# A spectral convolution with spline layers: who issues the copies of the modes

## The reference

```python
v  = groupnorm(x, 32 groups)                       # per image
ft = rfft2(v)
o[:, :, :16, :16]  = einsum('bixy,ioxy->boxy', ft[:, :, :16, :16],  w1)   # complex weights
o[:, :, -16:, :16] = einsum('bixy,ioxy->boxy', ft[:, :, -16:, :16], w2)
y  = irfft2(o) + einsum('bchw,oc->bohw', v, conv_w) + conv_b
y  = kan_linear(kan_linear(y, k1...), k2...)       # silu base + cubic splines over the channels
out = x + gelu(y)
```

## Time and profile before

| | us |
|---|---|
| median of 3 runs (3949.63 to 3950.17) | 3949.87 |
| the profiled execution, its own time | 3944.76 |
| its span in the trace | 3942.7 |
| TensorE busy | 3777.6 |
| VectorE busy | 3545.2 |
| ScalarE busy | 3421.6 |

### The profile page before, as it was taken

One profiled execution on the slowest core, in us unless ns is written; L12 is line 12 of the kernel. 1 busy time (PEld: TensorE's weight loads), 2 busy tenths in 40 slices (PEclk: granted clock), 3 DMA queues, 4 the chain that ended last, 5 costly groups with the idle time before them and its releaser, 6 DMA issues.

```text
span 3942.7 us, 102047 instructions
## 1 busy us (share of the span) xinstructions
PE 3777.6 (96%) x37098; PEld 2804.4 (71%) x37098; DVE 3545.2 (90%) x3979; ACT 3421.6 (87%) x3528; POOL 110.8 (3%) x132
## 2 busy tenths in 40 slices
PE   4995988999999999999999999999999999999998
PEld 2553944777777777777777777777777777777775
DVE  5774127999999999999999999999999999999996
ACT  1541227999999999999999999999999999999996
POOL 0000000000000000000000000000000000000000
PEclk9997999999999999999999999999999999999999
DMA  5996862322222332222222222322223222222322
GB/s 148 271 246 117 154 196 74 70 69 69 61 61 69 69 69 65 62 63 69 69 69 64 61 65 69 69 69 63 61 66 69 69 69 60 61 69 69 69 64 49
DMA packets 325155, 333.00 MB, mean 84 GB/s; under 512 B 86656, under 2 KB 255360, under 8 KB 323072
## 3 DMA queue, kind: packets, MB, share of 16 engines
q1 hardware_dynamic: 306688, 265.40, 24.9%
q0 software_dynamic: 18432, 67.12, 10.8%
HBM read 239.90 MB, written 88.08 MB: 83 GB/s over the span
## 4 chain that ended last, share of the span: by engine, by line
PE 83%; DVE 0%; issue 0%; ACT 0%; POOL 0%; POOLq 0%; ACTq 0%; DVEq 0%
PE l_ps L1092 78%; PE y_ps L1079 3%; PE y_ps L1071 2%; DVE cube2l L968 0%; DVE cube3r L968 0%; ACT above L1007 0%; ACT offset L1022 0%; ACT size L1018 0%; ACT S L1011 0%; ACT below L1015 0%; DVE cube1r L968 0%; DVE cube1l L968 0%; DVE cube0l L968 0%; ACT L1011 0%; DVE cube0r L968 0%
## 5 line engine op out<-in xcount | busy, mean ns | idle before, releaser
L1022 ACT ACTIVATE offset<-size 128x1024 f32<-128x1024 f32 x1280 | 1241.2, 1045 | 8.1
L1092 PE MATMUL l_ps<-S,kan_w 64*64 64x512 f32 x2048 | 358.2, 592 | 8.0 <-issue 8.0
L968 DVE SCALAR_TENSOR_TENSOR cube0r<-below,offset 128x1024 f32<-128x1024 f32 x256 | 312.1, 1219 | 58.5 <-ACT offset L1022 57.7
L1092 PE MATMUL l_ps<-below,kan_w 64*64 64x512 f32 x2048 | 359.2, 591 | 0.0
L1092 PE MATMUL l_ps<-cube3r,kan_w 64*64 64x512 f32 x2048 | 357.4, 589 | 0.8 <-DVE cube3r L968 0.8
L1092 PE MATMUL l_ps<-cube0r,kan_w 64*64 64x512 f32 x2048 | 358.0, 590 | 0.0
L1092 PE MATMUL l_ps<-cube0l,kan_w 64*64 64x512 f32 x2048 | 357.5, 589 | 0.0
L1092 PE MATMUL l_ps<-cube1l,kan_w 64*64 64x512 f32 x2048 | 357.5, 589 | 0.0
L1092 PE MATMUL l_ps<-cube1r,kan_w 64*64 64x512 f32 x2048 | 357.5, 589 | 0.0
L1092 PE MATMUL l_ps<-cube3l,kan_w 64*64 64x512 f32 x2048 | 357.4, 589 | 0.1
L1092 PE MATMUL l_ps<-inner_cube,kan_w 64*64 64x512 f32 x2048 | 357.4, 589 | 0.0
(11 more groups left out here) (129 smaller groups left out, 8106.6 us busy)
## 6 DMA issues: line engine op xcount, KB each, us to landing
img<-in_x_dram SPq DMA_DIRECT2D x128, 512.0 KB, 6.8
x_ring<-in_x_dram SPq DMA_DIRECT2D x256, 256.0 KB, 4.0
act_out<-in_x_dram POOLq DMA_DIRECT2D x128, 512.0 KB, 6.8
out_dram<-act_out SPq DMA_DIRECT2D x128, 512.0 KB, 2.6
rows_scratch<-rows SPq DMA_DIRECT2D x16, 1024.0 KB, 6.2
rows_t<-rows_scratch SPq DMA_DIRECT2D x512, 32.0 KB, 5.5
mix_w<-in_spec_w_r_dram SPq DMA_DIRECT2D x2, 2048.0 KB, 24.9
mix_w<-in_spec_w_i_dram SPq DMA_DIRECT2D x2, 2048.0 KB, 33.6
```

What stands on the lines that cost most here:

```text
L968: nc.vector.scalar_tensor_tensor(out=cube[q][side][:], in0=distance[layer][:], scalar=EDGE - KNOTS[q], in1=offset[layer][q][:], op0=ALU.mi ...
L1022: nc.scalar.activation(offset[layer][q][:], size[layer][:], ACT.Square, bias=-KNOTS[q]).then_inc(offset_ready[layer], 1)
L1092: ins = nc.tensor.matmul(dst[cols, r * MM:(r + 1) * MM], kan_w[layer][rows_, f, :], src[rows_, n * MM:(n + 1) * MM], start=(f == 0), stop= ...
```

## The change

The four DMAs A, B, C and D are taken out of SyncE's list and put at the head of ScalarE's list in the same block, in the same order and with the same semaphores. SyncE keeps the loads r0, i0, r1, i1. Nothing else differs.

```diff
         @block.sync
         def _(sp):
             sp.dma_start(pick_sb[:], t["pick"]).then_inc(pick_loaded, 16)
-            for k, ss in enumerate((slice(0, S_BANK), slice(S_BANK, NS))):
-
-                for part in range(2):
-                    src = modes[0:C, ss, :, part * MODES:(part + 1) * MODES, :]
-                    dst = modes[C:P, ss, :, (1 - part) * MODES:(2 - part) * MODES, :]
-                    sp.dma_start(dst.rearrange("p s g k b -> p (s g) (k b)"),
-                                 src.rearrange("p s g k b -> p (s g) (k b)")).then_inc(t["modes_doubled"][k], 16)
+            for k in range(2):
                 for part in range(2):
                     load_mix_part(nc, t, k, part, 0, C)
...
         @block.scalar
         def _(act):
+            for k, ss in enumerate((slice(0, S_BANK), slice(S_BANK, NS))):
+                for part in range(2):
+                    src = modes[0:C, ss, :, part * MODES:(part + 1) * MODES, :]
+                    dst = modes[C:P, ss, :, (1 - part) * MODES:(2 - part) * MODES, :]
+                    nc.scalar.dma_start(dst.rearrange("p s g k b -> p (s g) (k b)"),
+                                        src.rearrange("p s g k b -> p (s g) (k b)")).then_inc(t["modes_doubled"][k], 16)
             act.wait_ge(var_ready, 1)
             nc.scalar.activation(root[:], var[:], ACT.Sqrt).then_inc(root_ready, 1)
```

## The result

The changed kernel takes 3935.07 us (median of 7 runs, 3932.40 to 3940.25), the kernel before 3949.63 beside it (median of 7, 3943.62 to 3950.18). The ratio is 0.9968, with a 95% interval of 0.9956 to 0.998: 12.6 us less, from 8 to 17. The forecast was 3938.9. Times of the kernel before lie in two groups, near 3944 and near 3950, and its profiled execution (3944.76) is of the lower one; so the step by step account goes by the profiled executions, 3944.76 before and 3932.68 after.

The account below looks back on a forecast made before the run. It took the DMA engines' rate to bound `statistics`, through the landing of i1. Hiding r0's 12.0 us beside the copies, less 1.0 of friction, gave 3949.87 - 11.0 = 3938.9 us, range 3936.5 to 3950.5.

Parts of the forecast that it names:

- The bound: End of `statistics`: SyncE's issue of i1 comes last, released 17.9 us before i1 lands; the DMA rate bounds the stage.
- i and half of the r ahead of it: SyncE's issues in `statistics`: SyncE is released when this much transfer is still to come, 17.8 to 17.9 us.
- The rate: DMA in `statistics`: each half of the partitions takes some 180 to 190 GB/s of writes, both at once some 300.
- 276 GB/s: Copies beside r0 in `statistics`: the summed rate if each engine takes turns, r0 passing within the copies' 23.8 us.
- friction of 1.0 us: Copies beside the loads in `statistics`: 1.0 us of the gain lost if the copies go 4% slower.
- term of 11.0 us: r0 hidden beside the copies in `statistics`: up to 12.0 us, taken as 11.0, so i1 lands at 405.2.
- the first stores' wait: Stores of `mixed` behind i1 in `mix_modes`: TensorE's 3.26 us stall stays, since landing and start move equally.
- 2.8 us for the four issues: ScalarE issuing A to D at the head of `statistics`: 2.8 us unhindered, at cost 0.
- cover of 13 us: ScalarE in `statistics`: issues and table load end at 347.1, the square root's input comes at 360.15.
- "unhindered" 2.37 for r0: SyncE's issue of r0 in `statistics`: 2.37 us taken as an unhindered load, against 15.27 for i0 and 16.18 for i1.
- No overlap of worth: Rival, DMA in `statistics`: total rate stays 176 to 190 GB/s, time 3949.9; little or no overlap had chance 0.34.
- slower rival: Rival, DMA in `statistics`: turning between two queues brings the mixed stream below 176 GB/s; 3959.6 at 0.17 us; chance 0.04.

Follow-up runs that it names:

- e1_i_first: The changed kernel with the imaginary part of each chunk loaded ahead of the real one; 3948.26 us, ratio 1.0002 to the kernel before.
- e3: The changed kernel with r1 and i1 issued by SyncE at the head of `mix_modes`, not in `statistics`; 3933.50 us, ratio 0.9963.
- e4: Number not spelled out; by order, the changed kernel with r1, i1 issued in `mix_modes` and stores of `mixed` issued by ScalarE; 3931.30 us, ratio 0.996.

## Why the prediction was right

- *The bound.* Right: SyncE's last issue, i1, held the block, and it followed i1's landing: 17.6 us ahead of it after, 17.9 before. i0's distance became 20.6, for it was released while the queues were still sharing. In bytes it is the same: when i0's issue ended, 3.18 MB of SyncE's queue were still to be moved up to its landing, before and after, and for i1 3.31 before and 3.25 after. The predicted "i and half of the r ahead of it" is 3.15 MB.
- *The rate.* Right, and e1_i_first shows it: 282 GB/s beside a load into the other half, 185 to 195 beside one into the same. The "276 GB/s" came out as 287 to 291 in the three stretches of 4 us from 352 to 364. The engines do take turns between the queues, one packet each (761 against 759). Beside the load the copies moved at 190 GB/s, so the friction of 1.0 us, which had no row behind it, was not there.
- *The size.* The term of 11.0 us (12.0 less friction) measured 9.7. What was mis-sized is how much of r0 meets a copy. A, 1024 of the 4352 KB, ran alone. The 3328 KB left pair, one packet to one, with 1664 of r0's 2048 KB, which is 12.0 x 0.81 = 9.75 us. The other packets of r0 passed alone: some 500 as it came in (531 against 36 of ScalarE's queue from 349.5 to 350.5), the rest in the 0.7 us between D's landing and r0's. I had let both queues start together, which no row showed.
- *What follows behind.* The forecast let the first stores' wait move along unchanged; it went from 3.26 to 2.88. Right in its number, but the emphasis on the start of `mix_modes` was misplaced: e3 and e4 show that an earlier start alone is worth nothing. The sum held because the landing of i1 moved by the same amount as SyncE's release.
- *ScalarE.* The 2.8 us for the four issues was wrong: they took 12.23, D alone 8.18. The cover of 13 us took it in, with little to spare: the root came at 359.22, having still waited 3.26 for its input. SyncE's "unhindered" 2.37 for r0 was not unhindered either; with nothing ahead of it in the queue the issue took 0.68. With r0 first the four took 17.1, the table load and the root followed at once at 364.07, and the cover was gone; it still cost nothing, since the block ended only near 396.
- *The sum.* 9.66 in `statistics` and 0.38 in the wait make 10.0. The rest of the 11.8 us between the spans is 0.6 in `forward`, 0.6 in `inverse_rows` (first product to `y_ps`: 77.2 before, 76.6 after) and 0.6 scattered; no part of the change touches these, and the repeat does not have them all. The forecast of 3938.9 is 3.8 above the median mostly for the two groups of times: 3949.87 was of the upper one. How near the medians came to the forecast is in part chance; the stage itself gave 10.0 to 10.4 where 11.0 was forecast.
- *The rivals.* "No overlap of worth", with the rule of the Trainium skill, page "DMA: Bandwidth & Descriptors", section "Rules for kernel authors", that transfers to disjoint halves serialize, does not hold in these runs: 276 to 290 GB/s against 176 to 188. The port rule of the Trainium skill, page "SBUF — State Buffer", section "Door 1: The DMA port swizzle", fits these rates, though no run here shows a port. The slower rival needed an average under 176; the lowest in a stretch of 10 us with both queues at work was 183 (380 to 390 with r0 first).

## What to carry to other kernels

Look at which partitions a DMA writes. Two bulk transfers to the same half of the partitions shared 185 GB/s here, two to different halves 290, and it takes two queues to have them at work together (one queue that alternates in small pieces reached 215). Two queues took turns by the packet, so the one with packets of 1 KB moved twice as much as the one with 512 bytes. Pair them so that at each moment both halves are written, and count what is left over: here the queue per half was worth as much again as the change. And ask what the wait at the end of a block stands in for. If the first store behind it waits for the same transfers, starting earlier changes nothing.

## What the runs showed that I had not expected

- An issue can hold an engine much longer in a queue of its own than its size tells: D, 1152 KB, held ScalarE 8.18 us, where A (1024 KB) held it 0.70.
- A queue that comes second is not served at once: r0's data began to move only as A landed, about 7 us after the start of its issue.
- 290 GB/s is where the sum stops for packets of 512 bytes and 1 KB: images to all 128 partitions and two streams to opposite halves both stop there. It is not the most that the DMA engines move: in `inverse_rows`, where the packets are 5.8 KB on average (1689 for 9.75 MB), they move 325 over 30 us (last block below).
- The granted clock of TensorE in `inverse_rows` is not the same in each execution. The traced execution of e3_chunk1_late took 3940.07 us, its other runs 3932.5 to 3935.5. Its stretch from 545 to 575, and then that of the changed kernel:

```profile
545.00:575.00 30.00, 25.69 (x56) 10.83 (x54) 10.27 (x15) 8.36 (x14) 0.00 (x0) 0.94 0.75 261
```

```profile
545.00:575.00 30.00, 24.66 (x57) 10.30 (x56) 9.54 (x15) 8.36 (x14) 0.00 (x0) 1.00 0.94 325
```

The clock is 0.94 where it is 1.00 (it is at 1.2 GHz for part of the stretch), and from the first product of `inverse_rows` to `y_ps` it takes 82.2 us (518.64 to 600.83) and not 76.6. That is the size of the step between the two groups of times. The traced execution with r0 first is another such (3946.38, most others of that kernel 3940.0 to 3942.7): 81.9 us (525.04 to 606.95), with a clock of 0.84 from 544 to 574. No execution of the upper group of the kernel before was traced, but the mean clock of its runs was measured: in 52 runs of that kernel it is 0.985 in 18 of the 21 above 3947 and in none of the other 31, which have 0.986 or 0.987. So the upper group goes with a lower clock. What lowers it, and why the changed kernel is in that group more seldom, stays open.
